# A convolution block's 1x1 projections: f32 matmuls of a batch against three products of 16-bit halves, the halves of the input made by GpSimd

## What is computed

```
k = conv1x1(x, wk, bk); v = conv1x1(x, wv, bv); q = conv1x1(x, wq, bq)     # 256 -> 128 channels, n = 1024
attn = softmax(einsum('bcn,bcm->bnm', v, q), axis=2)
av   = einsum('bcn,bnm->bcm', k, attn)
y    = conv1x1(bn1(wwg @ av), wout, bout);  x = relu(bn2(y) + x)
t    = tokens(x);  t = t + attention(layernorm(t));  t = t + experts(layernorm(t))
```

## Time and profile before

| | us |
|---|---|
| median of 3 runs | 1183.61 (1182.93 to 1188.93) |
| span of the profiled execution | 1183.2 |
| TensorE busy | 1105.0 (93%) |
| VectorE busy | 818.8 (69%) |
| GpSimd busy | 600.2 (51%) |
| conv block, from the start to about | 250 |
| granted TensorE clock, 0 to 240 us | 1.00 |
| granted TensorE clock, mean of the span | 0.985 |

### The profile page before, as it was taken

One profiled execution on the slowest core, in us unless ns is written; L12 is line 12 of the kernel. 1 busy time (PEld: TensorE's weight loads), 2 busy tenths in 40 slices (PEclk: granted clock), 3 DMA queues, 4 the chain that ended last, 5 costly groups with the idle time before them and its releaser, 6 DMA issues.

```text
span 1183.2 us, 28483 instructions
## 1 busy us (share of the span) xinstructions
PE 1105.0 (93%) x10344; PEld 728.7 (62%) x10344; DVE 818.8 (69%) x1493; ACT 628.7 (53%) x1144; POOL 600.2 (51%) x513
## 2 busy tenths in 40 slices
PE   7999999978999999999999989898999999999995
PEld 4454645434444454555445545687899988989883
DVE  4666566766788788788878892768555656655773
ACT  3566676546677666766775665453333333333332
POOL 3424242314888763775477546167545445544540
PEclk9999999989999999999999999999999999999999
DMA  5356842626123230433243213723333233323328
GB/s 173 89 181 211 311 160 94 184 69 196 51 56 87 82 82 29 104 100 98 68 115 91 60 43 100 303 38 77 53 54 54 43 52 55 46 46 47 46 38 289
DMA packets 98884, 120.60 MB, mean 102 GB/s; under 512 B 29024, under 2 KB 76064, under 8 KB 98112
## 3 DMA queue, kind: packets, MB, share of 16 engines
q1 hardware_dynamic: 75280, 70.40, 20.3%
q0 software_dynamic: 20400, 42.08, 15.9%
q10 hardware_dynamic: 3072, 6.30, 1.5%
HBM read 73.10 MB, written 45.47 MB: 100 GB/s over the span
## 4 chain that ended last, share of the span: by engine, by line
PE 70%; DVE 11%; issue 6%; DMA 6%; ACT 3%; DVEq 3%; POOL 1%; SPq 1%; ACTq 0%; POOLq 0%
PE PP L1023 21%; PE PP L1448 11%; PE PP L1307 9%; PE PP L1333 8%; PE PP L1122 3%; DVE mxp L1739 3%; PE PP L1254 3%; PE PP L1194 3%; PE PP L1039 3%; PE PP L1322 2%; PE PP L1317 2%; DMA res_d<-WORK,lb 2%; PE PP L1154 1%; DVEq L2016 1%; DVE WORK L2017 1%
## 5 line engine op out<-in xcount | busy, mean ns | idle before, releaser
L953 ACT ACTIVATE WB<-PP 128x512 f32<-128x512 f32 x512 | 268.6, 606 | 146.1 <-PE PP L1333 146.0
L1739 DVE TENSOR_REDUCE mxp<-PP 128x2 f32<-128x1024 f32 x242 | 287.0, 1219 | 62.3 <-PE PP L1254 62.0
L993 ACT ACTIVATE WORK<-PP,b1c 128x256 f32<-128x256 f32 (+1 forms) x320 | 139.4, 450 | 239.4 <-PE PP L1023 191.7
L699 POOL TENSOR_TENSOR WB<-WB 128x1024 f32<-128x1024 f32 x84 | 197.8, 2358 | 89.4 <-PE PP L1322 58.7
L782 POOL DMA_INDIRECT res_d<-WORK,lb x70 | 117.6, 1680 | 157.8 <-DVE WORK L2034 144.7
L1448 PE MATMUL PP<-WB,WORK 128*128 x1704 | 193.8, 274 | 0.0
L1023 PE MATMUL PP<-WORK,WB 128*128 128x256 f16 (+1 forms) x1552 | 175.9, 273 | 2.4 <-DVE WORK L2003 1.7
L1448 PEld LDWEIGHTS PP<-WB,WORK 128*128 128x128 f16 x1704 | 165.2, 98 | 19.6
L1023 PE MATMUL PP<-WORK 128*128 128x128 f16 (+6 forms) x1086 | 161.1, 300 | 11.3 <-DVE WORK L1656 3.6
L1023 PEld LDWEIGHTS PP<-WORK,WB 128*128 (+1 forms) x1552 | 152.2, 102 | 22.2 <-issue 4.8
L1333 PE MATMUL PP<-WORK 97*128 97x256 f16 x1024 | 158.0, 277 | 6.7 <-ACT WB L953 4.2
(11 more groups left out here) (319 smaller groups left out, 1205.1 us busy)
## 6 DMA issues: line engine op xcount, KB each, us to landing
WORK<-in_L_ffn_W_dram POOLq DMA_DIRECT2D x32, 512.0 KB, 4.3
res_d<-WORK SPq DMA_DIRECT2D x8, 1024.0 KB, 5.2
late_d<-WB POOLq DMA_DIRECT2D x1, 6144.0 KB, 19.3
WB<-late_d ACTq DMA_DIRECT2D x3, 2048.0 KB, 14.0
v_d<-WORK SPq DMA_DIRECT2D x4, 1024.0 KB, 5.2
WORK<-q_hi_d SPq DMA_DIRECT2D x16, 256.0 KB, 3.7
WORK<-v_d SPq DMA_DIRECT2D x8, 512.0 KB, 5.6
WORK<-k_hi_d SPq DMA_DIRECT2D x16, 256.0 KB, 3.9
```

The costliest lines, as they stand in the source:

```text
L699: pool.tensor_tensor(PS[n % 2], PR[n % 3][:, 0], PR[n % 3][:, 1], ALU.add).then_inc(s("pair_kept"), 1)
L953: act.activation(PR[n % 3][:, c // 2, c % 2 * 2:c % 2 * 2 + 2], SCORES[m % 3] .rearrange("p (h n) -> p h n", h=2), ACT.Exp).then_inc(s("e_ ...
L993: act.activation(hid[:, k, 0:width], hidden_bank(k)[:, 0:width], ACT.Gelu, bias=b1c[:, bass.ds(e, 1), k], scale=1.0 / WSCALE)\
L1739: dve.tensor_reduce(mxp[:, n // 4 % 2, i, h:h + 2, k], PP[2 + h // 2][:, :].rearrange("p (h n) -> p h n", h=2), X_AXIS, ALU.max).then_inc( ...
```

## The change

An f16 copy of x in halves (`X16`: high, and the rest) and f16 halves of the three conv weights (`W16`) are added. Batch 0 is projected as before. For batches 1 to 3 GpSimd makes `X16`, two passes for each half of the channels, in its loop over weight parts ahead of part 5 of the batch before; VectorE makes `W16` once, in turn 0 behind the key scaling that follows the seventh maximum. Each f32 projection matmul of these batches becomes three f16 ones. TensorE waits for `x16_kept` in place of the load of x.

```diff
+        X16 = WB[:, E - LATE - 2].bitcast(F32)[:, 1536:3584].bitcast(F16).rearrange("p (d c n) -> p d c n", d=2, c=CC)
+        W16 = SPARE[:, 3 * N + P:3 * N + P + 768].bitcast(F16).rearrange("p (w n) -> p w n", w=2)
+        wq16, wv16, wk16 = [W16[:, :, 256 * i:256 * (i + 1)].rearrange("p w (c n) -> p w c n", c=CC) for i in range(3)]
...
-        wqT = take(256).rearrange("p (c n) -> p c n", c=CC)
-        wvT = take(256).rearrange("p (c n) -> p c n", c=CC)
-        kwT = take(256).rearrange("p (c n) -> p c n", c=CC)
+        QVKT = take(768)
+        wqT, wvT, kwT = [QVKT[:, 256 * i:256 * (i + 1)].rearrange("p (c n) -> p c n", c=CC) for i in range(3)]
...
+            def halves_of_x(n):
+
+                if n > 1:
+                    pool.wait_ge(s("k_made"), n)
+                for c in range(CC):
+                    pool.wait_ge(s(f"ld_{'xy'[n % 2]}{c}"), n // 2 * 16 + 16)
+                    pool.tensor_copy(X16[:, 0, c], XB[n][:, c])
+                    pool.drain()
+                    pool.tensor_tensor(X16[:, 1, c], XB[n][:, c], X16[:, 0, c], ALU.subtract)\
+                        .then_inc(s("x16_kept"), 1)
...
             for i, (e, _, at, gap) in enumerate(parts):
                 hi, lo = WB[:, e, at:at + HID], WB[:, e, at + gap:at + gap + HID]
+                if i % 8 == 5 and i // 8 + 1 < B:
+                    halves_of_x(i // 8 + 1)
                 pool.wait_ge(s("split_hi"), i + 1)
...
+            MEET = ((0, 0), (0, 1), (1, 0))
+
+            def project_half(n, dst, w, w16, c):
                 for h in range(2):
                     here = slice(h * HALF, (h + 1) * HALF)
-                    mm = pe.matmul(dst[:, here], w[:, c], XB[n][:, c, here], start=(c == 0), stop=(c == CC - 1))
+                    if n == 0:
+                        mm = pe.matmul(dst[:, here], w[:, c], XB[n][:, c, here], start=(c == 0), stop=(c == CC - 1))
+                        continue
+                    for i, (wd, xd) in enumerate(MEET):
+                        mm = pe.matmul(dst[:, here], w16[:, wd, c], X16[:, xd, c, here],
+                                       start=(c == 0 and i == 0), stop=(c == CC - 1 and i == 2))
                 return mm
 
             def project_q(n, c):
-                if c == 0 or not n:
-                    pe.wait_ge(s(f"ld_{'xy'[n % 2]}{c}"), n // 2 * 16 + 16)
+                if not n:
+                    pe.wait_ge(s(f"ld_x{c}"), 16)
+                else:
+                    pe.wait_ge(s("x16_kept"), 2 * n - 1 + c)
                 if n and not c:
                     pe.wait_ge(s("cv_kept"), 2 * n - 1)
-                    pe.wait_ge(s(f"ld_{'xy'[n % 2]}1"), n // 2 * 16 + 16)
+                    pe.wait_ge(s("w16_kept"), 1)
...
-                    product(PP[2][:, at], [(XB[n][:, c, at], kwT[:, c]) for c in range(CC)],
-                            "k_made" if t == NT - 1 else None)
+                    if n == 0:
+                        pairs = [(XB[n][:, c, at], kwT[:, c]) for c in range(CC)]
+                    else:
+                        pairs = [(X16[:, xd, c, at], wk16[:, wd, c]) for wd, xd in MEET for c in range(CC)]
+                    product(PP[2][:, at], pairs, "k_made" if t == NT - 1 else None)
...
+                        if b == 0 and i == 6:
+                            dve.tensor_copy(W16[:, 0], QVKT)
+                            dve.drain()
+                            dve.tensor_tensor(W16[:, 1], QVKT, W16[:, 0], ALU.subtract).then_inc(s("w16_kept"), 1)
```

More of the change, by code:

```diff
@@ L372, in hybrid_block @@
                      "tail_kept w1_kept fT_made f_out st_out0 st_out1 st_out2 st_out3 kone_kept t1_free lb_made wrc_kept wT_made wT_kept wp_made wp_kept "
-                     "early_kept gate_kept late_on nrm_last cnt_kept ld_f0 ld_f1 ld_f2 ld_f3 ld_f4 ld_f5 ld_f6 ld_f7 st_rows ld_l0 ld_l1 ld_l2 ld_l3 ld_l4 ld_l5 ld_last ones_kept").split():
+                     "x16_kept w16_kept early_kept gate_kept late_on nrm_last cnt_kept ld_f0 ld_f1 ld_f2 ld_f3 ld_f4 ld_f5 ld_f6 ld_f7 st_rows ld_l0 ld_l1 ld_l2 ld_l3 ld_l4 ld_l5 ld_last ones_kept").split():
             s(name)
@@ L1034, in _ @@
                 mm.then_inc(s("pe_prep"), 1)
-            def project_half(n, dst, w, c):
+            MEET = ((0, 0), (0, 1), (1, 0))
+            def project_half(n, dst, w, w16, c):
                 for h in range(2):
                     here = slice(h * HALF, (h + 1) * HALF)
-                    mm = pe.matmul(dst[:, here], w[:, c], XB[n][:, c, here], start=(c == 0), stop=(c == CC - 1))
+                    if n == 0:
[4 more added lines that the diff above has]
+                                       start=(c == 0 and i == 0), stop=(c == CC - 1 and i == 2))
                 return mm
             def project_q(n, c):
-                if c == 0 or not n:
-                    pe.wait_ge(s(f"ld_{'xy'[n % 2]}{c}"), n // 2 * 16 + 16)
+                if not n:
+                    pe.wait_ge(s(f"ld_x{c}"), 16)
+                else:
+                    pe.wait_ge(s("x16_kept"), 2 * n - 1 + c)
                 if n and not c:
                     pe.wait_ge(s("cv_kept"), 2 * n - 1)
-                    pe.wait_ge(s(f"ld_{'xy'[n % 2]}1"), n // 2 * 16 + 16)
-                mm = project_half(n, PP[0], wqT, c)
+                    pe.wait_ge(s("w16_kept"), 1)
+                mm = project_half(n, PP[0], wqT, wq16, c)
                 if c == CC - 1:
@@ L1055, in project_v @@
                 for c in range(CC):
-                    mm = project_half(n, PP[1], wvT, c)
+                    mm = project_half(n, PP[1], wvT, wv16, c)
                 mm.then_inc(s("v_made"), 1)
@@ L1409, in turn @@
                 mm.then_inc(s("xT_made"), 1)
-            MEET = ((0, 0), (0, 1), (1, 0))
             def first(t, u, e, wide=True):
```

## The result

| | before | after |
|---|---|---|
| median, us | 1184.05 (1182.93 to 1188.93, 4 runs) | 1211.65 (1206.64 to 1214.49, 4 runs) |
| span of the profiled execution | 1183.2 | 1212.6 |
| granted TensorE clock, mean of the span | 0.985 | 0.975 |

The medians are 27.6 us apart, the ratio is 1.022 with a 95% interval of 1.018 to 1.026: 26 us slower by the ratio, where 7 were forecast and 13 were the end of the range.

A forecast was written before the change was run, and what follows sets the result against it. TensorE, busy 93% of the span, bounds the kernel, with VectorE's branch setting the transposes. Late halves 2.5 plus lost clock 4.8 make 7.3 us slower: span 1190.5, time 1190.9 us, range 1185.3 to 1197.

The forecast's parts named there:

- GpSimd's halves: GpSimd's queue after the fifth weight part: copy, drain, subtraction ready 3.57 us after the DMA issue, late by 2.5 us altogether.
- dear ends: Rival: copy as long as the subtraction (5.4 us late) and more than one low-clock stretch per turn, 1195 to 1197; chance 0.15.
- GpSimd's copy of 128x1024: GpSimd's copy of one channel half of x to f16: 1.15 us, between 0.97 and 2.12.
- 48 key matmuls: TensorE's key projection from f16 halves: 2.86 us instead of 3.57, the gain going into the wait before the transposes.
- first projection, three halves: TensorE's first half of the query projection, three f16 products for one f32: 1.29 us instead of 1.72, on the path.
- late halves, three turns: TensorE's first projection waits for GpSimd: 1.45, 0.5 and 0.55 us after the 0.43 gain each, 2.5 in all.
- pause before L1173: TensorE's wait before the transposes, set by VectorE's branch, grows by 1.99 us to 2.95 us per turn.
- clock, three turns: TensorE's clock falls behind the longer wait before the transposes: 1.6 us per turn, 4.8 in all, the largest term.
- the clock holds: Rival: the wait before the transposes costs 0 instead of 4.8 us, 1186.1 us; chance 0.31 together with halves on time.
- The weights on VectorE: One weight split on VectorE, 1.5 us, delays the key scaling and makes the projection 1.7 us late, hidden, not added.
- The gain that isn't one: TensorE's projections: 1.99 us saved per turn goes into the wait before the transposes, since VectorE's branch of 9.7 us ends it.

The follow-up runs named there:

- the kernel with the semaphore: Kernel after, with GpSimd's drain between copy and subtraction replaced by a wait on the copy's own semaphore: 1189.98 us, ratio 1.0065.
- the drain alone: Kernel before, with only a one-column fill, a drain and another fill added at the three places in GpSimd's queue, no x split: 1176.34 us, one run.
- the later store: Kernel after, drain kept, with the 6 MB store issued after GpSimd's halves of batch 2 instead of ahead of them: 1201.04 us, ratio 1.0137.
- early halves: The kernel with the semaphore, with GpSimd's halves made a whole turn earlier and VectorE's weight split behind the last key scaling: 1189.58 us, ratio 1.0045.
- first half only: The kernel with early halves, but only the first half of the query projection from f16 halves, all other projections f32: 1181.76 us, ratio 0.9979.
- filled: The kernel with early halves, with five of eight key tiles of batches 1 to 3 made twice on TensorE: 1177.92 us, ratio 0.9949.
- VectorE off the path: Kernel before, transposes waiting for query and value low halves separately, router sums behind keys: 1177.05 us with f16 halves in batches 2 and 3, 1181.88 all f32.

## Why the prediction was wrong

*The step that failed* is the sentence on the drain in "GpSimd's halves": "The drain and the two semaphore steps are 0.3 together, by the 0.30 us that GpSimd stands between its subtraction and L649, and which may be half or double." The row stands for the handing over of a result by a semaphore. The drain waited for GpSimd's outstanding transfers, 2.84, 16.09 and 2.90 us. Of the 27.6 us that the medians are apart, this step holds 21.7, by the kernel with the semaphore. The prediction had gone through that queue by name, and what it needed was in the profile: the load of 51.15 is issued right ahead of the copy, a load from there takes 4.2 us to land, and a drain behind two such loads stands in the same trace with 8.1 us (L660, shown at the drain alone). It asked of the DMA issue only how long it holds the engine. None of its rivals had the drain; "dear ends", the nearest, stopped at 1197.

*What held*, in the kernel with the semaphore, which is the kernel that was predicted:

| step | forecast | measured |
|---|---|---|
| GpSimd's copy of 128x1024 | 1.15 (0.97 to 2.12) | 1.05 |
| 48 key matmuls | 2.86 | 2.84 |
| first projection, three halves | 1.29 | 1.47 |
| late halves, three turns | 2.5 | 2.2 (1.74, 0.22, 0.26) |
| pause before L1173 | 2.95 | 3.12, 3.05, 3.03 |
| clock, three turns | 4.8 (1.6 each) | 5.4 (1.5, 1.2, 2.7) |
| total | 1190.9 | 1190.0 |

The parts of the lateness are the steps of the token matmuls against before (55.67, 118.52, 181.29 and now 57.41, 122.00, 186.24), less the clock lost in the turn before; those of the clock are the growth from the start of L1200 to that of L1221 (3.09 where it holds) and of L1221 over 10.53. That the total is met to 0.9 us is in part luck. Lateness and clock make 7.6, the fourth batch is 6.0 late: the 1.6 between them is the clock that the kernel before loses behind its wait of 1.88 us at 242.44, and this one does not; the forecast had no such term, and its three latenesses (1.45, 0.5, 0.55) were each off.

*The clock* was the right mechanism and the rival "the clock holds" fell, though not everywhere: of twelve pauses of 3.0 to 3.1 us before L1200 (in the kernels after, with the semaphore, with the later store and with early halves) nine were followed by a low clock, and of eleven of 0.9 to 1.4 us (before, first half only, filled, VectorE off the path) not one. What sets the three apart I can't say; in two of them the token matmuls just ahead had been slow (5.38 and 5.39 us). By the Trainium skill (TensorE: Matmul & The Clock Gate, "HAM oscillation — how this bites in real kernels") the clock falls in long pauses between bursts; here pauses of 3 us were long enough nine times in twelve, and shorter ones with more work, in the filled kernel, never. What the prediction drew from the earlier trace rows, that even 1.88 us cost the clock, is weaker than it looked: of ten kernels with that wait six keep it, as the one with the fill does (its L1149 behind it takes 1.96 us, not 3.35). In the kernel after, the clock cost 5.3 us of the 29.2: 2.7 in the first turn, 2.9 in the second (projection 1.3, token matmuls 1.7), 1.3 in the third, less the same 1.6. In the second turn it was lost in the stop of 16 us:

```profile
132.00:136.00 4.00, 0.00 (x0) 0.00 (x0) 0.00 (x0) 0.00 (x0) 0.00 (x0) 0.50 0.79 324
...
140.00:144.00 4.00, 4.00 (x13) 2.53 (x14) 0.00 (x0) 0.00 (x0) 3.05 (x2) 0.50 0.62 218
```

These are stretches of the kernel after, columns as above: no engine works for 4 us, then TensorE's token matmuls run at 1.2 GHz (5.38 us for 3.71).

*The weights on VectorE* came as worked out (kernel after; forecast: scaling at 45.5, 1.7 us):

```profile
43.59 0.96 DVE L1672 TENSOR_TENSOR WB<-WORK,WB 128x768 f16<-128x768 f32 x1
...
45.83 1.71 DVE L1652 TENSOR_SCALAR WORK<-WORK,rinv 128x128 f32<-128x128 f32 x1
```

It was hidden behind the late halves but for the 0.3 us by which GpSimd's issue moved (51.15 to 51.44). The Trainium skill (SBUF — State Buffer, "Who interferes with whom") has one instruction hold the port for its whole length; the 1.71 us here and the 1.31 and 2.07 us for small instructions in the early kernels agree.

*The gain that isn't one.* That 1.99 of TensorE's 2.42 us a turn would go into the pause held in every kernel that left VectorE's branch as it was: pauses of 0.9 us with f32 matmuls and 3.0 to 3.1 with f16, and the value of the halves came out (1.4 us in two turns) only after that branch was cut.

*Left open.* The span behind the fourth batch's transposes is 913 to 916 us long in four of the profiles (semaphore 914.3, fill 914.2) and 918 to 921 in six (before 920.7, after 920.9, early 918.5), and no edit goes with it. It makes 4.2 of the 9.5 us between the profiled executions without and with the fill, and 7.5 of the 8.7 by which the span of the one run of the drain alone lies under that of the kernel before. Each is one execution, so how much of the 11.7 us by medians comes from there isn't known. The milestones of the stage don't depend on it.

## What to carry to other kernels

Before a drain is put on an engine that also issues transfers, list its transfers that are still on the way, the big store first: between a producer and a consumer on GpSimd a semaphore of the producer cost 0.1 us here, the drain as long as the last of its transfers needed to land. An engine made faster ahead of a wait that another sets only waits longer, and on TensorE that was worse than nothing here: find the branch that ends the wait and cut it, and only then give TensorE less to do. A wait that the profile calls only "issue", like the drain's, stands as idle time before the engine's next instruction: look there for a drain that the kernel already has, and ask what it waits for before asking how long it takes.

## What the hardware showed that was not expected

- GpSimd's drain ended 0.4 to 0.7 us after the last transfer issued by GpSimd had landed, whatever stood ahead of it. The wait was 0.15 us with none on the way, 2.8 to 3.8 with a 512 KB load issued right before, 16 to 17 with a load queued behind a 6 MB store. A load of SyncE's on its way did not hold it (0.16 us).
- The 512 KB load behind that store took 17.4 us to land, and 4.2 where the store came later.
- TensorE's clock at half speed behind a pause of 3 us cost 1.2 to 2.7 us each time it happened (nine times in twelve), and with 1.7 us of useless matmuls in each pause it did not happen.
- A GpSimd copy of 128x1024 from f32 to f16 takes 1.05 us, half of the two-input subtraction of the same size (2.12).
- After a wait of 1.88 us, the same in ten kernels, the clock fell in four and held in six, and no edit goes with it.
